# Two entries moved in a handwritten order: a transpose ahead of its neighbour, and a scaling behind the layernorm statistics

## The reference

```python
q, k, v = (proj(wq), proj(wk), proj(wv))
q = (q @ fq1_w.T + fq1_b) * (q @ fq2_w.T + fq2_b)
k = (k @ fk1_w.T + fk1_b) * (k @ fk2_w.T + fk2_b)
...
kv = cumsum(kc^T vc) without its own chunk;  inter = qc @ kv;  intra = tril(qc @ kc^T) @ vc
o = (inter + intra).reshape(B, H, L, dk)
o = o * jax.lax.rsqrt(jnp.mean(o * o, axis=-1, keepdims=True) + EPS) * norm_w
x = _layernorm(x + o @ wo.T)
```

## Time and profile before

| | |
|---|---|
| median of 3 runs | 1619.34 us (1618.8 to 1619.4) |
| the profiled execution | 1618.8 us, its span 1617.1 us |
| PE busy in the span | 1507.2 us (93%) |
| DVE, ACT, POOL busy | 1030.4, 723.1 and 341.3 us (64%, 45%, 21%) |
| the chain that ended last | PE 60%, issue 23%, DVE 9%, POOL 4%, ACT 3% |

### The profile page before, as it was taken

One profiled execution on the slowest core, in us unless ns is written; L12 is line 12 of the kernel. 1 busy time (PEld: TensorE's weight loads), 2 busy tenths in 40 slices (PEclk: granted clock), 3 DMA queues, 4 the chain that ended last, 5 costly groups with the idle time before them and its releaser, 6 DMA issues.

```text
span 1617.1 us, 24158 instructions
## 1 busy us (share of the span) xinstructions
PE 1507.2 (93%) x9681; PEld 1038.9 (64%) x9681; DVE 1030.4 (64%) x1993; ACT 723.1 (45%) x1005; POOL 341.3 (21%) x256
## 2 busy tenths in 40 slices
PE   7899999999999988899999999987889999988998
PEld 5677777777778765344555555455556666556887
DVE  3335455454645465977677776753899888645665
ACT  3333333233333323976786777642233343442333
POOL 0011212121211131000000000000466767750001
PEclk9999999999999999999999999998899999999999
DMA  6011120203030151000100110012100000000112
GB/s 226 29 47 52 51 77 26 77 26 102 2 102 30 28 183 41 6 27 27 52 29 24 53 53 1 1 65 80 37 1 1 0 1 1 0 1 27 53 53 78
DMA packets 43483, 71.51 MB, mean 44 GB/s; under 512 B 7035, under 2 KB 14715, under 8 KB 43244
## 3 DMA queue, kind: packets, MB, share of 16 engines
q1 hardware_dynamic: 43372, 69.97, 12.9%
HBM read 44.80 MB, written 25.17 MB: 43 GB/s over the span
## 4 chain that ended last, share of the span: by engine, by line
PE 60%; issue 23%; DVE 9%; POOL 4%; ACT 3%; SPq 1%; DMA 1%; DVEq 0%; POOLq 0%; ACTq 0%
PE psum L142 12%; PE psum L143 12%; PE psum L144 12%; PE psum L1319 5%; PE psum L614 2%; PE psum L640 2%; PE psum L635 2%; PE psum L629 2%; PE psum L649 2%; PE psum L988 1%; PE psum L1297 1%; PE psum L981 1%; DVE c_mx L1235 1%; PE psum L653 1%; PE psum L644 1%
## 5 line engine op out<-in xcount | busy, mean ns | idle before, releaser
L981 PE MATMUL psum<-early,high 128*128 128x512 fp8e4 x1024 | 241.1, 388 | 23.1 <-DVE low_r L953 15.8
L981 PEld LDWEIGHTS psum<-early,high 128*128 128x128 fp8e4 x1024 | 99.0, 99 | 147.1 <-DVE low_r L953 17.2
L406 POOL TENSOR_TENSOR rms<-ms,mhalf 128x16 f32<-128x16 f32 x32 | 94.7, 2959 | 408.5 <-DVE ms L476 408.5
L1174 POOL TENSOR_TENSOR c_ls<-c_ls,c_pr 128x512 f32<-128x512 f32 (+2 forms) x136 | 161.3, 1186 | 63.9 <-ACT c_pr L1211 55.1
L1211 ACT ACTIVATE c_pr<-c_sc 128x512 f32<-128x512 f32 (+2 forms) x144 | 85.3, 594 | 173.7 <-DVE c_sc L1255 158.6
L142 PE MATMUL psum<-Qh,Kh 128*128 128x512 f32 (+1 forms) x272 | 143.7, 528 | 1.8 <-DVE Ql_r L1528 1.8
L1319 PE MATMUL psum<-c_pr,V 128*128 128x512 f32 (+2 forms) x288 | 139.6, 567 | 3.5 <-ACT c_pr L1211 3.4
L1255 DVE TENSOR_TENSOR c_sc<-psum,c_mb 128x512 f32<-128x512 f32 (+2 forms) x144 | 91.9, 640 | 45.9 <-PE psum L144 35.0
L988 PE MATMUL psum<-high,b_act 128*128 128x512 fp8e4 x512 | 115.3, 379 | 0.0
L565 ACT ACTIVATE early<-psum 128x512 f32<-128x512 f32 x64 | 38.3, 598 | 158.4 <-PE psum L144 158.4
L142 PE MATMUL psum<-early_r,high_r 128*128 128x512 f32 x256 | 105.6, 413 | 3.3 <-DVE early_r L439 3.3
(11 more groups left out here) (243 smaller groups left out, 3358.6 us busy)
## 6 DMA issues: line engine op xcount, KB each, us to landing
low<-x_dram SPq DMA_DIRECT2D x9, 1024.0 KB, 5.7
xs<-in_L_attn_x SPq DMA_DIRECT2D x8, 1024.0 KB, 7.6
wst<-in_L_ffn_w_gating SPq DMA_DIRECT2D x16, 512.0 KB, 4.1
x_dram<-xs SPq DMA_DIRECT2D x7, 1024.0 KB, 4.9
x_dram<-low SPq DMA_DIRECT2D x5, 1024.0 KB, 4.3
wst<-in_L_ffn_w_linear SPq DMA_DIRECT2D x16, 256.0 KB, 4.5
high<-x_dram SPq DMA_DIRECT2D x4, 1024.0 KB, 6.7
out<-high SPq DMA_DIRECT2D x4, 1024.0 KB, 4.3
```

The source lines that it names most:

```text
L406: nc.gpsimd.tensor_tensor(rms[:, :], ms[:, :], const["mhalf"][:, 0:H], ALU.pow).then_inc(*done)
L981: last = t.matmul(out[:, h, :], w8g[:, tile + k, (2 * m + h) * P:(2 * m + h + 1) * P], x8[:, u, k, :], start=k == 0, stop=k == DC - 1)
L1174: nc.gpsimd.tensor_tensor(ls[:, i % 2, q0:], ls[:, i % 2, q0:], pr[:, g % SLOTS, q0:], ALU.add).then_inc(*L.done(*name))
```

## The change

Two edits, each to where something stands in an order; no operation is added, removed or altered. The entry `("r", b, 2)` moves ahead of `("k2", f)` in the list of a repetition, and `on` is placed one job ahead of its `oT` and no longer two.

```diff
-                    ("s", b, 2), ("st", b, 2), ("kt", b, 3), ("k", f, 3), ("oT", b, 1), ("o", b, 2), ("k1", f), ("v", f, 2), ("k2", f), ("r", b, 2),
+                    ("s", b, 2), ("st", b, 2), ("kt", b, 3), ("k", f, 3), ("oT", b, 1), ("o", b, 2), ("k1", f), ("v", f, 2), ("r", b, 2), ("k2", f),
                     ("v", f, 3), ("s", b, 3), ("st", b, 3), ("y", b, 1), ("oT", b, 2), ("o", b, 3)]
...
-            ahead = next(((x[1], x[2]) for x in order[n + 2:n + 3] if x[0] == "oT"), None)
+            ahead = next(((x[1], x[2]) for x in order[n + 1:n + 2] if x[0] == "oT"), None)
             if ahead:
                 dve_order.append(("on", *ahead))
```

## The result

The changed kernel takes 1658.12 us (median of 4 runs, 1655.27 to 1660.53) against 1619.07 for the kernel before on the same chip (1617.44 to 1619.40). The ratio is 1.0238, with a 95% interval of 1.0225 to 1.0250: slower, by 39 us. The profiled execution took 1657.51 us, its span 1655.8.

A forecast was written before the change was run, and what follows sets the result against it. TensorE was taken as the bound, without a gap in the repetitions, so each new wait adds to the total: 1618.8 + 27.6 (waits) + 9.0 (clock falls) = 1655.4, 1656 us with 0.5 to the median; range 1646 to 1662.

The forecast's parts named there:

- `r` ahead of `k2`: On VectorE sum and `eps` delay `kf`, so `s` on TensorE waits 0.98 us in 7 repetitions (bounds 0.5 to 1.4).
- `on` behind the group: In 7 repetitions `on` follows the group of `y` piece 1; `oT` of piece 2 starts 3.71 us later, 2.73 new.
- The eighth repetition and the last piece: `oT` of piece 2 in the eighth repetition starts 2.0 us later; the last piece's `y` gains 0.4 us.
- The clock: Half-speed stretches on TensorE follow 6 of 8 possible idle times, 1.5 us each, 9.0 us (bounds 0 and 12).
- its own last sentence: Wrong in mechanism if `oT` lacks the wait; in size if `s` never waits or clock falls never or always.
- The first (a clock that mostly holds): Both TensorE waits come, but the clock falls none to two times: 1647 to 1650 us; chance 18%.
- The second (only one wait): `kf`'s delay is hidden or the square comes early: 1640 us with no fall, 1649 with six; chance 7%.
- The third (`kf` kept out by `rms`): GpSimd's `rms` keeps out `kf`'s second step; `s` starts 2.9 us later, 20 us more, 1676 us; chance 3%.
- The fourth (not slower): `on` is released early enough by an earlier `rms`, no new waits arise, 1.5 us won, 1618 us; chance 3%.

The follow-up runs named there:

- the first edit alone: Kernel before with only `r` of piece 2 moved ahead of `k2`, `on` placed as before: 1624.69 us, ratio 1.0031.
- the second edit alone: Kernel before with only `on` moved to one job ahead of its `oT`, `r` behind `k2` as before: 1648.25 us, ratio 1.0182.

## Why the prediction was right

The forecast was 1656 us, the measured median 1658.1.

**`r` ahead of `k2`.** Forecast 0.98 us at `s`, in 7 repetitions; the trace shows 0.90 at `s` and the first edit alone 0.80 for a whole repetition. The steps were those I had named: `kf` starts 2.78 us behind `r`, where I had 2.76. Only `s` follows the end of `kf` by 0.06 us and not by the 0.15 that I had taken from `on` and `oT`. That the loss is VectorE's order and not TensorE's is shown by putting `kf` first again.

**`on` behind the group.** Forecast 2.73 us, measured 2.73. Filling the wait, shortening it to 1.47 us and covering it with `o` each moved the time as this predicts.

**The eighth repetition and the last piece.** Forecast +2.0 and -0.4. Measured are 3.00 - 1.09 = +1.9 at the eighth `oT` of piece 2, and for the last piece -0.64 at `y` and +0.22 at `oT`, -0.4 together. (The delay is 39.68 us at the eighth `oT` and 40.86 at the last `y`, with a fall of 1.60 us between.)

**The clock.** Forecast six falls of 8, at 1.5 us: 9.0. The profiled execution had all 8, at 1.60 us: 12.8, above the 12 us that I had as the upper bound. By its own last sentence the prediction was wrong in its size here, since the clock fell every time. The mechanism (an idle time of this size, then half speed) holds, the number of falls doesn't. I had taken it from the share of like idle times that a fall follows, 5 of 7. The trace of the kernel before has nine of 2.6 to 2.8 us that begin at full clock, and a fall follows seven of them, which gives six of 8 as well. The base was wrong: the same 2.61 us brought 4, 4, 7, 7 and 3 falls of 7 in five kernels. Other idle times fit no order of length either: one of 1.51 us (with the idle time filled, at 665.10) and one of 1.88 us were followed by a fall, that of 2.16 us was not the earlier trace rows, and neither was one of 3.08 us (the first edit alone, at 590.27).

The sum for the profiled execution: 7 x (0.80 + 2.73) = 24.7, + 1.9 - 0.4 for the end, + 12.8 for eight falls, makes 39.0. A fall in the eighth repetition that lasted twice as long adds about 1.0, the start of the stage 0.9, and the later stages give back 2.2 us. That is 38.7, and 1657.5 - 1618.8 = 38.7.

That the total came within 2.1 us is in part luck. The waits were 1.4 us less than forecast (26.2 against 27.6) and the falls 3.8 us more, and 1.9 us at places that the prediction didn't look at were nearly made up by the 2.2 us of the later stages.

**The rivals.** The first (a clock that mostly holds) is refuted by the trace. The second (only one wait) by the first edit alone. The third (`kf` kept out by `rms`) by the trace: 2.47 us for both steps beside `rms`. The fourth (not slower) by every run with both edits: with an `rms` that ended at 363.45, VectorE reached `on` only at 369.72.

## What to carry to other kernels

Where an engine is busy without a gap, read what stands directly ahead of each instruction it will wait for, on the other engine's list: a step placed "one job later" can end up behind a group that itself waits for the engine's last product, and then the wait is the whole length of that group. Reordering pays where the trace has idle time (here the last repetition, 0.7%), and not where a result merely comes earlier. And a wait of 1.5 to 3 us on TensorE should be priced twice: once for itself, and once for the half-speed stretch that may follow it, 1.4 to 1.6 us in these repetitions. Whether it follows can't be read off the length of the wait, so the bounds of such a forecast are no fall and a fall every time.

## What the runs showed of the hardware that I had not expected

A loop seems to be able to fall into step with the clock. With both edits, and with the second edit and four more products, the repetitions settle at 78.5 us and every one has a fall; with the second edit alone (76.1 us without a fall) it is every second one. In the kernel with the second edit and four more products the first repetitions last 78.63 and 78.61 us and the last 78.51, though each has the same idle time, and in its last three the falls sit at the same place, to a few hundredths; the fifth and sixth (columns as above):

```profile
448.51:454.13 5.62, 3.02 (x20) 2.81 (x24) 3.01 (x6) 0.60 (x1) 0.93 (x1) 0.71 0.00 0
527.01:532.63 5.62, 3.01 (x21) 2.80 (x24) 3.01 (x6) 0.60 (x1) 0.92 (x1) 0.71 0.00 0
```

That loop and clock are in step is my reading of these equal distances; no run tests it by itself. What is measured is that adding work to such a loop can be nearly free, as the change with four more products shows (1658.88 against 1658.12 us).

GpSimd's `rstd`, a power of one column, takes 0.55 us in the kernel before, and 0.93 us in each of the seven repetitions of the changed kernel, where it starts at 369.88 while VectorE runs `on` (369.72 to 370.40). `on` reads both its inputs from SBUF; beside `kf`, which reads a tile from PSUM, one from SBUF and a column of scalars from SBUF, `rms` kept its 2.92 us. The Trainium skill (page "SBUF — State Buffer", section "SBUF: two separate sides") says that a VectorE instruction with two inputs in SBUF and a GpSimd instruction that reads SBUF hold each other up, and that the one which starts second waits. These rows agree, with GpSimd as the one that is held (it ends at 370.81, 0.41 us behind the end of `on`), and show that the column of scalars did not count as a second input. It cost nothing here, since nobody waited for `rstd`.
